# Half-wide gathered rows and an accumulating scatter in the expert part of a Macaron block

## The chip, the cores and the metric

The kernel runs on one core of a Trainium2 chip, in one launch. The metric is the device time of that core in microseconds (us).

## The reference, cut to what matters

The block computes x + 0.5 ffn(ln(x)), then adds causal attention with a relative bias, then adds 0.5 ffn(ln(x)) again, on 8192 tokens of 256 channels in float32. Both ffn calls have the same weights. One ffn is:

```python
y1 = _ln(x + _mha(x, ...), ln1_g, ln1_b)
y2 = _ln(y1 + _moe(y1, wg, w1, b1, w2, b2), ln2_g, ln2_b)   # then out = x + 0.5 * y2
# _moe: token -> its best of 8 experts, at most 1024 tokens each; others get 0
h = einsum('ecd,edf->ecf', disp, w1) + b1
y = einsum('ecf,efd->ecd', h, w2) + b2
out = where(keep, gate_val * y[slot], 0.0)
```

There is no nonlinearity between w1 and w2, so the kernel folds each expert into one 256x256 matrix.

## The kernel before, in words

`macaron` (L2422) runs `ffn` (turn 0, from the input to the scratch tensor x1), three stages of the causal attention, and `ffn` again (turn 1, from x2 to the output). Each stage ends with a barrier over the engines.

`ffn` (L943) has three parts.

1. `ffn_attention` (L295) goes over 16 groups of 512 tokens. It computes y1 and the router's logits. On GpSimd, `x_ahead` (L884) adds the halved ln2_b to the block's input. SyncE stores two things in token order into `rows`, a DRAM scratch tensor of 8192 rows of 2C floats: y1 into the first C columns (L340) and that residual part into the last C (L344).
2. VectorE works out a slot for every token (L1351 to L1435), sorted by expert, and with TensorE (L1271) its inverse `inv`: which token sits in slot i. In turn 0 alone, TensorE folds the weights meanwhile: `turn_w1` (L1238) and `product` (L1250) for each of 8 experts, from w1 and w2 tiles that SyncE loads; VectorE computes `bias_product` (L1441), ScalarE evacuates. In turn 1 the folded weights are loaded.
3. The expert loop goes over 16 groups of 4 tiles of 128 slots. GpSimd first issues all 64 gathers (L1094): each is one indirect DMA that fetches 128 rows of `rows`, 2 KB a row, by `inv` into the buffer `xs`. Then it issues 64 scatters (L1112), four when a group is finished (`s_fin`), each writing 128 rows of 1 KB to the result by `inv`. ScalarE copies the gathered y1 (`place`, L1147), evacuates its transpose (L1155), seeds the PSUM banks with the bias (L1162), takes the root (L1169) and normalises (L1173). TensorE transposes (L1228) and multiplies (L1321). VectorE adds the gated expert result and takes statistics (`sums`, L1463), the factors (L1487), and in `scale` (L1496) multiplies by ln2_g (L1498) and adds the gathered residual part (L1501). The order on VectorE in step n is sums(n), factors(n-1), scale(n-2). The first two and last two steps are unrolled, the middle is a hardware loop over pairs.

The first TensorE work behind the weights is L1318, which marks the PSUM banks; the loop can't start before it.

`xs` holds 16 groups of GT*2C floats in each partition, 128 KB. Before the gathers it is lent out: groups 0 to 7 to part 1 and to the tables of the inverse, 8 and 9 to the slot computation, 10 to 15 to the w1 and w2 tiles. So in turn 0 the gathers of groups 10 to 15 wait for the folding:

```python
for n in range(NG):
    if turn == 0 and n in (10, 11):
        pool.wait_ge(s_etps, 4 * (n - 3))
    if turn == 0 and n >= 12:
        pool.wait_ge(s_w12ps, n - 7)
        pool.wait_ge(s_acc, n - 7)
    gather(n)
```

`gather(n)` also waits until the gathers of group n-2 have landed. Before the first gather GpSimd waits until all stores of part 1 have landed (`stored`, L922), and behind the last scatter until all scatters have (L1114).

Of the kernel before, what the change touches and what calls it, by code (L numbers as in the profile page):

```python
# [291 lines left out]
            nc.tensor.transpose(core.ps[:, 7, 0:NE * FB], b1raw[:, :], core.ident[0:NE * FB, 0:NE * FB]).then_inc(s_b1ps, 1)  # L292


def ffn_attention(core, ph, lend, x, rows, logits, first, tables, early_loads):  # L295


    nc = core.nc
    xg = x.rearrange("(p t) c -> p (t c)", p=P)
    rowsg = rows.rearrange("(p t) c -> p t c", p=P)  # L300
    wide, kv, xs, ys, back = lend
    qT = wide.take(2, 2, GW)
    xin, xb, xres = (wide.take(2, GT, C) for _ in range(3))
# [35 lines left out]
    def sync(sp):  # L339
        def store(n, u):  # L340
            sp.wait_ge(s_y1, n + 1)
            sp.dma_start(rowsg[:, bass.ds(n * GT, GT), 0:C], y1[:, u, :, :]).then_inc(s_store[u], 16)

        def ahead(n, u):  # L344
            sp.wait_ge(s_xb, n + 1)
            sp.dma_start(rowsg[:, bass.ds(n * GT, GT), C:2 * C], xb[:, u, :, :]).then_inc(s_ahead[u], 16)

        def body(n, u):
            if not under(n, 2):
                sp.wait_ge(s_xres, n - 1)  # L350
                sp.wait_ge(s_xTps, 2 * n - 2)
            sp.dma_start(xin[:, u, :, :].rearrange("p t c -> p (t c)"),
                         xg[:, bass.ds(n * GT * C, GT * C)]).then_inc(s_load[u], 16)
            if not under(n, 1):
                ahead(n - 1, 1 - u)
            if not under(n, 4):
                store(n - 4, u)
            if n == NG - 1:
                early_loads(sp)
            if first and 2 <= n < 2 + len(tables):  # L360
                sp.dma_start(*tables[n - 2]).then_inc(core.tables, 16)
        each(NG, body)
        ahead(NG - 1, (NG - 1) % 2)
        for n in range(NG - 4, NG):
            store(n, n % 2)
        for u in range(2):
            sp.wait_ge(s_store[u], 16 * (NG // 2))
            sp.wait_ge(s_ahead[u], 16 * (NG // 2))
# [574 lines left out]
def ffn(core, name, x, rows, d, w12d, b12d, out, turn, tables):  # L943

    nc = core.nc
    FB = FF // P
    CT = TILES // NG * 2
    MINE = (2, 5)  # L950
    with Phase(core, name) as ph:
        logits = ph.sb("logits", [P, TILES, NE])

        def tile(n, *shape, dt=F32):
            return ph.sb(n, [P, *shape], dt)
        mx, se, first, keep, loc, rank, drop, dscan, t2, t3 = (tile(n, TILES) for n in (
            "mx", "se", "first", "keep", "loc", "rank", "drop", "dscan", "t2", "t3"))
        xs = ph.sb("xs", [P, NG, GT, 2 * C])
        flat = xs[:, :, :, :].rearrange("p g t c -> p (g t c)")
        ROWS = GT * 2 * C  # L960

        def lent(k, *shape):

            n, k = int(np.prod(shape)), int(k * ROWS)
            names = "abc"[:len(shape)]
            return flat[:, k:k + n].rearrange(f"p ({' '.join(names)}) -> p {' '.join(names)}", **dict(zip(names, shape)))

        CHUNKS = TILES // CT
        onb, ona = lent(0, CHUNKS, CT, P), lent(4, CHUNKS, CT, 2 * TILES)
        dif, ex, cand = (lent(8 + i / 4, TILES, NE) for i in range(3))  # L970
        hot, scan, a3, b3 = (lent(9 + i / 4, NE, TILES) for i in range(4))
        w1 = [lent(10 + i, KB, FF) for i in range(2)]
        w2 = [lent(12 + i, FB, C) for i in range(4)]
        onest = tile("onest", TILES)
        eidx, ebase, tot, cnt, free, fend, fbeg, off = (tile(n, NE) for n in (
            "eidx", "ebase", "tot", "cnt", "free", "fend", "fbeg", "off"))
# [28 lines left out]
                                                   ("rs", [P, 2, GT]), ("nb", [P, 2, GT])))  # L1005
        s_got, s_sent = core.indirect[0:2], core.indirect[2]
        got0, sent0 = turn * 16 * TILES // 2, turn * 16 * TILES
        s_tps, s_tsb, s_zps, s_sum, s_st, s_mv, s_ve, s_sd, s_inv2, s_rs, s_norm, s_scaled, s_fin, s_marked, s_seed = (
            ph.sem(x) for x in ("tps", "tsb", "zps", "sum", "st", "mv", "ve", "sd", "inv2", "rs", "norm", "scaled", "fin",
                                "marked", "seed"))  # L1010
        gnow = ph.sb("gnow", [P, 2, GT])
        s_gnow, s_mine, s_y1 = ph.sem("gnow"), ph.sem("mine"), ph.sem("y1")
# [31 lines left out]
        def load_w1(sp, e):  # L1044
            if e >= 2:
                sp.wait_ge(s_etps, 4 * (e - 1))
            sp.dma_start(w1[e % 2], d["L0_ffn_w1"][e, :, :].rearrange("(k p) f -> p k f", p=P)).then_inc(s_w1[e % 2], 16)

        def load_w2(sp, e):
            if e >= 4:  # L1050
                sp.wait_ge(s_w12ps, e - 3)
                sp.wait_ge(s_acc, e - 3)
            sp.dma_start(w2[e % 4], d["L0_ffn_w2"][e, :, :].rearrange("(k p) c -> p k c", p=P)).then_inc(s_w2[e % 4], 16)

        lend = (Lent(flat[:, 0:7 * ROWS]), Lent(w12[:, :, :].rearrange("p k c -> p (k c)")),
                Lent(xT[:, :, :, :].rearrange("p u k c -> p (u k c)")),
                Lent(y1[:, :, :, :].rearrange("p u t c -> p (u t c)")), Lent(flat[:, 7 * ROWS:8 * ROWS]))
        attend_sync, attend_tensor, attend_scalar, attend_vector, attend_gpsimd, over_yet, stored = ffn_attention(
            core, Phase(core, name + "_a", ph), lend, x, rows, logits, turn == 0, tables, early_loads)
        block = ph.block()  # L1060

        @block.sync
# [18 lines left out]
        @block.gpsimd  # L1081
        def _(pool):
            nc.gpsimd.iota(ei[:, :], pattern=[[1, NE]], base=0, channel_multiplier=0).then_inc(s_iota, 1)
            nc.gpsimd.iota(ib[:, :], pattern=[[1, P]], base=0, channel_multiplier=0).then_inc(s_ib, 1)
            nc.gpsimd.iota(ni[:, :], pattern=[[1, TILES]], base=0, channel_multiplier=TILES).then_inc(s_ni, 1)
            nc.gpsimd.memset(zero[:, :], 0.0).then_inc(s_zero, 1)
            attend_gpsimd(pool)

            def gather(n):
                if n >= 2:  # L1090
                    got(pool, n - 2, n % 2)
                for t in range(GT):
                    i = n * GT + t
                    pool.indirect_dma_start(xs[:, n, t, :], None, rows,  # L1094
                                            bass.IndirectOffsetOnAxis(ap=inv[:, i:i + 1], axis=0)
                                            ).then_inc(s_got[n % 2], 16)

            for u in range(2):
                stored(pool, u)
            pool.wait_ge(s_inv, 1)  # L1100
            for n in range(NG):
                if turn == 0 and n in (10, 11):
                    pool.wait_ge(s_etps, 4 * (n - 3))
                if turn == 0 and n >= 12:
                    pool.wait_ge(s_w12ps, n - 7)
                    pool.wait_ge(s_acc, n - 7)
                gather(n)
            for n in range(NG):
                pool.wait_ge(s_fin, n + 1)
                for t in range(GT):  # L1110
                    i = n * GT + t
                    pool.indirect_dma_start(out, bass.IndirectOffsetOnAxis(ap=inv[:, i:i + 1], axis=0),  # L1112
                                            xs[:, n, t, 0:C], None).then_inc(s_sent, 16)
            pool.wait_ge(s_sent, sent0 + 16 * TILES)  # L1114

        @block.scalar
# [226 lines left out]
        def _(dve):  # L1343
# [152 lines left out]
            def scale(n):  # L1496
                wait_apart(dve, s_norm, n + 1)
                nc.vector.tensor_tensor(all_rows(n, 0, C), all_rows(n, 0, C), over(core.rows["ln2_g"][:, :], GT, 1),  # L1498
                                        ALU.mult).then_inc(s_scaled, 1)
                wait_apart(dve, s_scaled, n + 1)  # L1500
                nc.vector.tensor_tensor(all_rows(n, 0, C), all_rows(n, 0, C), all_rows(n, C, 2 * C), ALU.add).then_inc(s_fin, 1)  # L1501

            def body(n, u):
                sums(n, u)
# [917 lines left out]
def macaron(nc, d, out):  # L2422
    def scratch(name, shape, dt=F32):
        return nc.dram_tensor(name, shape, dt, kind="Internal").ap()

    x = d["L0_attn_x"].rearrange("b t c -> (b t) c")
    y = out.rearrange("b t c -> (b t) c")
    x1, x2 = (scratch(n, (S, C)) for n in ("x1", "x2"))
    rows = scratch("rows", (S, 2 * C))
    w12d, b12d = scratch("w12d", (P, KB * NE * C)), scratch("b12d", (P, NE * C))  # L2430
    qd, kd = (scratch(n, (B * C, 3, T), BF16) for n in ("qparts", "kparts"))
    relrow = scratch("relrow", (AH, 2, 3 * P))
    neard = scratch("neard", (AH, P, PITCH))
    neardT = scratch("neardT", (AH, P, PITCH))
    lowd = scratch("lowd", (2 * B * NHG, LOW_PARTS, HG * T // 2), BF16)
    with ExitStack() as ctx:
        core = Core(nc, ctx)
        prepare(core, d, relrow)
        ffn(core, "ffn1", x, rows, d, w12d, b12d, x1, 0, distance_tables(relrow, neard, neardT))
        with Phase(core, "attention") as ph:  # L2440
            vall = ph.sb("vall", [P, B * NHG, QB, HG * AD])
            attention_qkv(core, x1, qd, kd, vall)
            attention_core(core, qd, kd, neard, neardT, lowd, vall)
            attention_out(core, x1, vall, x2)
        ffn(core, "ffn2", x2, rows, d, w12d, b12d, y, 1, ())
# [27 lines left out]
```

## Time and profile before

| | us |
|---|---|
| median of 3 runs | 2800.32 (2793.59 to 2802.8) |
| the profiled execution's own time | 2796.27 |
| its span | 2794.5 |
| busy: PE, DVE, ACT, POOL | 2350.3, 2150.2, 1657.6, 818.8 |
| indirect DMA issues on POOL: gathers, scatters | 122.8, 130.4 |

In the rows, POOL is GpSimd, DVE VectorE, ACT ScalarE, PE TensorE (PEld its weight loads) and SP SyncE. A row of a timeline has its start, its duration, the engine, the line, the operation, what it writes and reads, how often it stands there, and in brackets the idle time before it and what ended it. "issue" is time in which the engine waited for nothing that the profile shows.

### The profile page before, as it was taken

The numbers are of one execution on the slowest core, as the hardware profiler recorded it, in microseconds if no ns is written. First come the engines' busy times: TensorE is split into PE (matmuls) and PEld (weight loads), VectorE is DVE, ScalarE is ACT, GpSimd is POOL, SyncE is SP. The second block draws the span as 40 slices with busy tenths as digits, with TensorE's granted clock in tenths as the row PEclk, the third lists the DMA queues.
The fourth block names the chain that finished last, engine by engine and source line by source line (L and its number), as shares of the span: only waits on it lengthen the run. The fifth ranks groups of instructions, "written<-read, shape, count | busy, mean of one in ns | idle before, by whom it ended". The sixth has DMA issues, their size and how long they took to land. (4 is left out here: it accounts for less than half of the span.)

```text
span 2794.5 us, 47798 instructions
## 1 busy us (share of the span) xinstructions
PE 2350.3 (84%) x15864; PEld 1424.9 (51%) x15864; DVE 2150.2 (77%) x5653; ACT 1657.6 (59%) x3995; POOL 818.8 (29%) x853
## 2 busy tenths in 40 slices
PE   5999998867479969999999999999869999984263
PEld 4666665746345514444444444444646666663243
DVE  5888887727778869888898988997448888886076
ACT  3455453416534429999999999999215545442154
POOL 2243443263634420000000000000223344331735
PEclk8999999878789969999999999999989999996677
DMA  4132213382235464454554544542441121111712
GB/s 119 53 98 73 69 56 134 133 259 94 79 128 172 160 130 102 93 109 99 101 109 91 105 104 96 111 94 44 139 140 54 46 69 53 61 52 55 210 62 73
DMA packets 244680, 281.50 MB, mean 101 GB/s; under 512 B 41809, under 2 KB 212881, under 8 KB 243809
## 3 DMA queue, kind: packets, MB, share of 16 engines
q1 hardware_dynamic: 218192, 218.81, 30.7%
q0 software_dynamic: 16384, 50.35, 5.7%
q10 hardware_dynamic: 9872, 9.45, 1.0%
q8 instruction: 123, 2.02, 0.3%
q14 instruction: 109, 0.88, 0.1%
HBM read 190.63 MB, written 94.16 MB: 102 GB/s over the span
## 5 line engine op out<-in xcount | busy, mean ns | idle before, releaser
L2208 DVE CUSTOM_DVE_ANT_0 banks<-banks,attn_bias 128x128 f32<-128x128 f32 (+7 forms) x1024 | 759.9, 778 | 109.1 <-PE banks L1917 83.3
L2121 ACT ACTIVATE attn_probT<-banks 128x512 f32<-128x512 f32 x1152 | 622.6, 621 | 61.7 <-PE banks L1934 51.4
L1917 PE MATMUL banks<-attn_kst,attn_qst 96*128 96x512 bf16 (+3 forms) x1536 | 421.9, 336 | 22.9 <-DMA attn_kst<-kparts 12.7
L1934 PE MATMUL banks<-attn_qst,attn_kst 99*128 99x256 bf16 (+3 forms) x2176 | 410.8, 281 | 15.0 <-ACT attn_probT L2121 6.8
L1956 PE MATMUL banks<-attn_probT,attn_vb 128*32 128x256 f32 (+3 forms) x4352 | 316.0, 400 | 7.7 <-ACT attn_probT L2121 7.3
L1934 PEld LDWEIGHTS banks<-attn_qst,attn_kst 99*128 99x128 bf16 x2176 | 187.8, 98 | 168.5 <-ACT attn_probT L2121 54.5
L2266 POOL CAST attn_lowp<-attn_lowT 128x32 bf16<-128x32 f32 x64 | 13.4, 209 | 851.4 <-DVE attn_lowT L2216 851.4
L421 PE MATMUL banks<-ffn_xT,winT 128*128 128x512 f32 x512 | 250.9, 613 | 6.0 <-ACT ffn_w L621 2.9
L1917 PEld LDWEIGHTS banks<-attn_kst,attn_qst 96*128 96x128 bf16 x1536 | 117.5, 97 | 257.3 <-DVE attn_low L2208 159.2
L2109 ACT COPY banks<-attn_biasT 128x512 f32<-128x512 f32 x384 | 227.8, 628 | 28.3 <-DMA attn_biasT<-neardT 21.7
L881 POOL TENSOR_TENSOR ffn_xs<-ffn_xs,row_ffn_out 128x1024 f32<-128x1024 f32 x32 | 75.3, 2354 | 413.6 <-DVE ffn_xs L763 387.1
L591 ACT ACTIVATE ffn_xs<-banks,ffn_xs 128x128 f32<-128x128 f32 x512 | 182.4, 379 | 13.0 <-DVE ffn_xs L728 11.6
L1956 PEld LDWEIGHTS banks<-attn_probT,attn_vb 128*32 128x32 f32 x4352 | 106.2, 109 | 132.8 <-ACT attn_probT L2121 69.9
L630 ACT COPY ffn_xs<-banks 128x256 f32<-128x256 f32 x128 | 48.2, 377 | 203.6 <-PE banks L470 200.2
L1329 PE MATMUL banks<-ffn_w,ffn_xT 128*128 (+1 forms) x512 | 135.0, 419 | 40.3 <-issue 30.3
L1094 POOL DMA_INDIRECT ffn_xs<-rows,ffn_inv x128 | 122.8, 960 | 146.8 <-DVE ffn_inv L1435 94.1
L621 ACT ACTIVATE ffn_w<-banks,ffn_qk_b 64x512 f32<-64x512 f32 x128 | 87.3, 682 | 128.7 <-PE banks L421 127.9
L728 DVE TENSOR_REDUCE ffn_xs<-banks 128x4 f32<-128x512 f32 x128 | 88.5, 691 | 89.7 <-PE banks L450 89.7
L450 PEld LDWEIGHTS banks<-ffn_w,ffn_xs 128*128 128x128 f32 x1024 | 133.8, 198 | 23.7 <-issue 20.3
L450 PE MATMUL banks<-ffn_w,ffn_xs 128*128 128x128 f32 x1024 | 143.6, 285 | 0.8 <-DVE ffn_xs L750 0.8
L2208 DVE DVE_READ_ACCUMULATOR2_ANT attn_low<- 128x1 f32 x1024 | 144.3, 141 | 0.0
L736 DVE TENSOR_SCALAR ffn_xs<-ffn_xs 128x128 f32<-128x128 f32 x512 | 137.8, 331 | 4.5
(254 smaller groups left out, 4489.5 us busy)
## 6 DMA issues: line engine op xcount, KB each, us to landing
rows<-ffn_xs SPq DMA_DIRECT2D x64, 512.0 KB, 3.1
attn_qst<-qparts SPq DMA_DIRECT2D x384, 64.0 KB, 2.8
attn_kst<-kparts SPq DMA_DIRECT2D x192, 128.0 KB, 4.9
ffn_xs<-in_L_ffn_w_dram SPq DMA_DIRECT2D x16, 1024.0 KB
attn_biasT<-neardT SPq DMA_DIRECT2D x128, 128.0 KB, 4.9
attn_bias<-neard SPq DMA_DIRECT2D x128, 128.0 KB, 2.2
qparts<-qkv_part SPq DMA_DIRECT2D x32, 384.0 KB, 2.8
kparts<-qkv_part SPq DMA_DIRECT2D x32, 384.0 KB, 2.8
```

The source lines that it names most:

```text
L421: mm = nc.tensor.matmul(bank[QK], core.winT[:, k, j * P:(j + 1) * P], xT[:, u, k, :], start=(k == 0), stop=(k == KB - 1))
L450: mm = nc.tensor.matmul(bank[SC[t % 2]][:, h * P:(h + 1) * P], qT[:, u, h // 2, t * P:(t + 1) * P], kT[:, u, h, t * P:(t + 1) * P], start= ...
L591: ins = nc.scalar.activation(prob[:, t % 2, h, :], bank[SC[t % 2]][:, h * P:(h + 1) * P], ACT.Exp, bias=negm[:, t % 2, h:h + 1], scale=1.0 ...
L736: ins = nc.vector.tensor_scalar(prob[:, t % 2, h, :], prob[:, t % 2, h, :], rinv[:, t % 2, h:h + 1], None, ALU.mult)
L1094: pool.indirect_dma_start(xs[:, n, t, :], None, rows, bass.IndirectOffsetOnAxis(ap=inv[:, i:i + 1], axis=0)).then_inc(s_got[n % 2], 16)
L1329: mm = nc.tensor.matmul(part, xT[:, u, k, t * P:(t + 1) * P], w12[:, k, expert(n, u)], start=False, stop=(k == KB - 1), skip_group_check=True)
L1917: mm = nc.tensor.matmul(score[k % 2][:, a:e], qst[0:K6, u, half, hh, ii * P:(ii + 1) * P], kst[0:K6, u, hh, a:e], start=True, stop=True)
L1934: mm = nc.tensor.matmul(tbank[t % 3][:, at:at + nb * P], kst[:, u, hh, j * P:(j + 1) * P], qst[:, u, half, hh, x:x + nb * P], start=(k == ...
L1956: mm = nc.tensor.matmul(obank[32 * hh:32 * hh + 32, x:x + nb * P], vb[:, u, j, hh, :], probT[:, g % 2, i, at:at + nb * P], start=hh not in ...
L2109: nc.scalar.copy(tbank[t % 3].rearrange("p (a c) -> p a c", a=2), over(near[:, 0:2 * P], 2, 1)).then_inc(s_seed, 1)
L2121: nc.scalar.activation(probT[:, g % 2, i, 0:w], tbank[t % 3][:, 0:w], ACT.Exp, scale=-1.0).then_inc(s_exp, 1)
L2208: nc.vector.tensor_tensor_reduce(out=part, in0=part, in1=bias[:, hh, T - w:T], scale=1.0, scalar=BIG, op0=ALU.add, op1=ALU.min, accum_out= ...
```

## The change

`rows` has C columns and holds y1 alone. The residual part is stored in token order to the result of the ffn itself (x1 in turn 0, the output in turn 1). The gathers fetch 1 KB a row. VectorE's addition L1501 is gone with its semaphore. The scatters add to the result in DRAM instead of overwriting it. `xs` has half the size, and the tiles of the slot computation and of w1 and w2 are allocated beside it, so the waits of turn 0 ahead of the gathers of groups 10 to 15 are gone. The tables of the inverse still lie in `xs`.

```diff
-            sp.dma_start(rowsg[:, bass.ds(n * GT, GT), 0:C], y1[:, u, :, :]).then_inc(s_store[u], 16)
+            sp.dma_start(rowsg[:, bass.ds(n * GT, GT), :], y1[:, u, :, :]).then_inc(s_store[u], 16)
-            sp.dma_start(rowsg[:, bass.ds(n * GT, GT), C:2 * C], xb[:, u, :, :]).then_inc(s_ahead[u], 16)
+            sp.dma_start(outg[:, bass.ds(n * GT, GT), :], xb[:, u, :, :]).then_inc(s_ahead[u], 16)
...
-        xs = ph.sb("xs", [P, NG, GT, 2 * C])
+        xs = ph.sb("xs", [P, NG, GT, C])
...
-        onb, ona = lent(0, CHUNKS, CT, P), lent(4, CHUNKS, CT, 2 * TILES)
-        dif, ex, cand = (lent(8 + i / 4, TILES, NE) for i in range(3))
-        hot, scan, a3, b3 = (lent(9 + i / 4, NE, TILES) for i in range(4))
-        w1 = [lent(10 + i, KB, FF) for i in range(2)]
-        w2 = [lent(12 + i, FB, C) for i in range(4)]
+        before_rows = Lent(flat)
+        onb, ona = before_rows.take(CHUNKS, CT, P), before_rows.take(CHUNKS, CT, 2 * TILES)
+        dif, ex, cand = (tile(n, TILES, NE) for n in ("dif", "ex", "cand"))
+        hot, scan, a3, b3 = (tile(n, NE, TILES) for n in ("hot", "scan", "a3", "b3"))
+        w1 = [tile(f"w1_{i}", KB, FF) for i in range(2)]
+        w2 = [tile(f"w2_{i}", FB, C) for i in range(4)]
...
             for n in range(NG):
-                if turn == 0 and n in (10, 11):
-                    pool.wait_ge(s_etps, 4 * (n - 3))
-                if turn == 0 and n >= 12:
-                    pool.wait_ge(s_w12ps, n - 7)
-                    pool.wait_ge(s_acc, n - 7)
                 gather(n)
...
-                                            xs[:, n, t, 0:C], None).then_inc(s_sent, 16)
+                                            xs[:, n, t, :], None, compute_op=ALU.add).then_inc(s_sent, 16)
...
                 nc.vector.tensor_tensor(all_rows(n, 0, C), all_rows(n, 0, C), over(core.rows["ln2_g"][:, :], GT, 1),
-                                        ALU.mult).then_inc(s_scaled, 1)
-                wait_apart(dve, s_scaled, n + 1)
-                nc.vector.tensor_tensor(all_rows(n, 0, C), all_rows(n, 0, C), all_rows(n, C, 2 * C), ALU.add).then_inc(s_fin, 1)
+                                        ALU.mult).then_inc(s_fin, 1)
...
-    rows = scratch("rows", (S, 2 * C))
+    rows = scratch("rows", (S, C))
```

## Rows read from the trace of the kernel before

**Rows 1.** Engines' busy time by stretch; then granted clock, DMA share, GB/s

```profile
core 0: us, PE busy (x) PEld busy (x) DVE busy (x) ACT busy (x) POOL busy (x), PEclk, DMA share, GB/s
50.00:500.00 450.00, 410.71 (x2508) 287.95 (x2508) 370.16 (x1023) 218.16 (x754) 174.58 (x91) 0.97 0.26 82
580.00:600.00 20.00, 10.41 (x22) 5.03 (x20) 0.00 (x0) 0.00 (x0) 15.13 (x17) 0.50 0.75 223
2607.00:2617.00 10.00, 0.00 (x0) 0.00 (x0) 0.00 (x0) 0.00 (x0) 7.56 (x9) 0.50 0.72 207
2657.00:2667.00 10.00, 2.93 (x5) 1.15 (x4) 1.04 (x3) 0.00 (x0) 0.59 (x1) 0.50 0.20 59
2677.00:2757.00 80.00, 59.23 (x274) 47.41 (x273) 71.06 (x199) 57.43 (x112) 42.73 (x44) 0.93 0.20 72
```

**Rows 2.** Timeline of POOL, turn 1: first and last gather, first and last scatter

```profile
2577.76 1.09 POOL L1094 DMA_INDIRECT ffn_xs<-rows,ffn_inv  x1 [47.20 <-DVE ffn_inv L1435]
...
2656.65 0.95 POOL L1094 DMA_INDIRECT ffn_xs<-rows,ffn_inv  x1 [0.30 <-issue]
2678.54 1.00 POOL L1112 DMA_INDIRECT out_dram<-ffn_xs,ffn_inv  x1 [20.95 <-DVE ffn_xs L1501]
...
2786.10 0.97 POOL L1112 DMA_INDIRECT out_dram<-ffn_xs,ffn_inv  x1 [0.30 <-issue]
```

**Rows 3.** Timeline of POOL, turn 0: first and last gather, first and last scatter

```profile
540.65 1.44 POOL L1094 DMA_INDIRECT ffn_xs<-rows,ffn_inv  x1 [46.85 <-DVE ffn_inv L1435]
...
635.46 0.95 POOL L1094 DMA_INDIRECT ffn_xs<-rows,ffn_inv  x1 [0.30 <-issue]
659.19 1.01 POOL L1112 DMA_INDIRECT x<-ffn_xs,ffn_inv  x1 [22.78 <-DVE ffn_xs L1501]
...
765.52 0.97 POOL L1112 DMA_INDIRECT x<-ffn_xs,ffn_inv  x1 [0.30 <-issue]
```

**Rows 4.** A piece of the chain of waits, turn 1: start, us, what

```profile
2603.50 19.10 issue
```

**Rows 5.** Timeline of DVE, two steps of the expert loop

```profile
2700.71 0.16 DVE L1466 COPY ffn_gnow<-ffn_gates 128x4 f32 x1
...
2705.32 1.23 DVE L1498 TENSOR_TENSOR ffn_xs<-ffn_xs,row_ln_g 128x1024 f32 x1
2706.74 1.23 DVE L1501 TENSOR_TENSOR ffn_xs<-ffn_xs  x1 [0.20 <-issue]
2707.89 0.16 DVE L1466 COPY ffn_gnow<-ffn_gates 128x4 f32 x1
...
2714.95 0.16 DVE L1466 COPY ffn_gnow<-ffn_gates 128x4 f32 x1
```

**Rows 6.** Timeline of ACT, the same step

```profile
2704.96 0.21 ACT L1171 ACTIVATE ffn_ve<-ffn_ve 128x4 f32<-128x4 f32 x1 [1.67 <-issue]
...
2709.28 1.10 ACT L1166 COPY banks<-ffn_b 128x512 f32 x2
```

**Rows 7.** DMA queue of the gathers, 2577 to 2667: packets, MB, share

```profile
q0 software_dynamic: 5120, 16.78, 64.6%
```

**Rows 8.** DMA queue of the scatters, 2677 to 2757: packets, MB, share

```profile
q0 software_dynamic: 2112, 5.77, 20.3%
```

**Rows 9.** Timeline of PE, turn 1: the first products of the loop

```profile
2593.31 4.93 PE L1329 MATMUL banks<-ffn_w,ffn_xT 128*128 128x256 f32 x16
```

**Rows 10.** Timeline of PE, turn 0: three products, the banks' marks

```profile
548.26 7.07 PE L1257 MATMUL banks<-ffn_xs,ffn_xT 128*128 128x256 f32 x32
...
568.53 7.07 PE L1257 MATMUL banks<-ffn_xs,ffn_xT 128*128 128x256 f32 x32
...
611.59 7.07 PE L1257 MATMUL banks<-ffn_xs,ffn_xT 128*128 128x256 f32 x32
...
633.21 5.40 PE L1318 MATMUL banks<-ffn_w,ones 128*128 128x512 f32 x8 [0.56 <-issue]
```

**Rows 11.** Timeline, all engines: a scatter's issue beside VectorE's product

```profile
2761.79 1.22 DVE L1498 TENSOR_TENSOR ffn_xs<-ffn_xs,row_ln_g 128x1024 f32<-128x1024 f32 x1
2761.85 1.99 POOL L1112 DMA_INDIRECT out_dram<-ffn_xs,ffn_inv  x1 [0.30 <-issue]
```

More of the change, by code:

```diff
@@ L292, in _, with ffn_attention @@
             nc.tensor.transpose(core.ps[:, 7, 0:NE * FB], b1raw[:, :], core.ident[0:NE * FB, 0:NE * FB]).then_inc(s_b1ps, 1)
-def ffn_attention(core, ph, lend, x, rows, logits, first, tables, early_loads):
+def ffn_attention(core, ph, lend, x, rows, out, logits, first, tables, early_loads):
     nc = core.nc
     xg = x.rearrange("(p t) c -> p (t c)", p=P)
-    rowsg = rows.rearrange("(p t) c -> p t c", p=P)
+    rowsg, outg = (a.rearrange("(p t) c -> p t c", p=P) for a in (rows, out))
     wide, kv, xs, ys, back = lend
@@ L957, in ffn @@
             "mx", "se", "first", "keep", "loc", "rank", "drop", "dscan", "t2", "t3"))
-        xs = ph.sb("xs", [P, NG, GT, 2 * C])
+        xs = ph.sb("xs", [P, NG, GT, C])
         flat = xs[:, :, :, :].rearrange("p g t c -> p (g t c)")
[L960 to L966, printed above, removed]
-        CHUNKS = TILES // CT
-        onb, ona = lent(0, CHUNKS, CT, P), lent(4, CHUNKS, CT, 2 * TILES)
-        dif, ex, cand = (lent(8 + i / 4, TILES, NE) for i in range(3))
-        hot, scan, a3, b3 = (lent(9 + i / 4, NE, TILES) for i in range(4))
-        w1 = [lent(10 + i, KB, FF) for i in range(2)]
-        w2 = [lent(12 + i, FB, C) for i in range(4)]
+        CHUNKS = TILES // CT
+        before_rows = Lent(flat)
[4 more added lines that the diff above has]
+        w2 = [tile(f"w2_{i}", FB, C) for i in range(4)]
         onest = tile("onest", TILES)
@@ L1007, in ffn @@
         got0, sent0 = turn * 16 * TILES // 2, turn * 16 * TILES
-        s_tps, s_tsb, s_zps, s_sum, s_st, s_mv, s_ve, s_sd, s_inv2, s_rs, s_norm, s_scaled, s_fin, s_marked, s_seed = (
-            ph.sem(x) for x in ("tps", "tsb", "zps", "sum", "st", "mv", "ve", "sd", "inv2", "rs", "norm", "scaled", "fin",
+        s_tps, s_tsb, s_zps, s_sum, s_st, s_mv, s_ve, s_sd, s_inv2, s_rs, s_norm, s_fin, s_marked, s_seed = (
+            ph.sem(x) for x in ("tps", "tsb", "zps", "sum", "st", "mv", "ve", "sd", "inv2", "rs", "norm", "fin",
                                 "marked", "seed"))
@@ L1046, in load_w1 @@
                 sp.wait_ge(s_etps, 4 * (e - 1))
-            sp.dma_start(w1[e % 2], d["L0_ffn_w1"][e, :, :].rearrange("(k p) f -> p k f", p=P)).then_inc(s_w1[e % 2], 16)
+            sp.dma_start(w1[e % 2][:, :, :], d["L0_ffn_w1"][e, :, :].rearrange("(k p) f -> p k f", p=P)).then_inc(s_w1[e % 2], 16)
         def load_w2(sp, e):
@@ L1052, in load_w2 @@
                 sp.wait_ge(s_acc, e - 3)
-            sp.dma_start(w2[e % 4], d["L0_ffn_w2"][e, :, :].rearrange("(k p) c -> p k c", p=P)).then_inc(s_w2[e % 4], 16)
-        lend = (Lent(flat[:, 0:7 * ROWS]), Lent(w12[:, :, :].rearrange("p k c -> p (k c)")),
+            sp.dma_start(w2[e % 4][:, :, :], d["L0_ffn_w2"][e, :, :].rearrange("(k p) c -> p k c", p=P)).then_inc(s_w2[e % 4], 16)
+        LATE = 2 * GT * C
+        lend = (Lent(flat[:, :-LATE]), Lent(w12[:, :, :].rearrange("p k c -> p (k c)")),
                 Lent(xT[:, :, :, :].rearrange("p u k c -> p (u k c)")),
-                Lent(y1[:, :, :, :].rearrange("p u t c -> p (u t c)")), Lent(flat[:, 7 * ROWS:8 * ROWS]))
+                Lent(y1[:, :, :, :].rearrange("p u t c -> p (u t c)")), Lent(flat[:, -LATE:]))
         attend_sync, attend_tensor, attend_scalar, attend_vector, attend_gpsimd, over_yet, stored = ffn_attention(
-            core, Phase(core, name + "_a", ph), lend, x, rows, logits, turn == 0, tables, early_loads)
+            core, Phase(core, name + "_a", ph), lend, x, rows, out, logits, turn == 0, tables, early_loads)
         block = ph.block()
```

## The prediction

> **What bounds the kernel now.** I read the stage table first. In part 1 of an ffn TensorE is busy 411 of 450 us [rows 1]; the change adds or takes nothing on TensorE there, so I look only at the stretch behind `inv`, in both turns. The timeline of POOL cuts it in two. In turn 1 the 64 gathers go out back to back from 2577.8 to 2657.6, one in 1.25 us; the first scatter follows only at 2678.5, and the last issue ends at 2787.07, 108.5 us later, though 64 scatters at 1.275 us (0.97 and 0.30 of gap) take 81.6 [rows 2]. In turn 0 gathers run from 540.7 to 636.4, scatters from 659.2 to 766.5, 107.3 us [rows 3].
>
> Why are the scatters late? While gathers run, the other engines nearly stop: between 2607 and 2617 PE, DVE and ACT run nothing, with DMA 72% busy at 207 GB/s; in turn 0 from 580 to 600 DVE and ACT none [rows 1]. The chain of waits has a piece of 19.1 us there that it calls "issue" [rows 4]: nothing that the trace shows is awaited. I read this as instructions that don't arrive. Afterwards the expert loop runs at DVE's pace, 71 busy of 80 us [rows 1], one step in 7.18 us here [rows 5] (7.12 as the mean of two neighbours), and POOL waits for each group.
>
> **L1501 goes.** From the start of L1498 to that of L1501 is 1.42 us, so a step of DVE falls from 7.12 to 5.70 [rows 5]. Next in line are ACT, 5.42 us from its root to the end of its seeds [rows 6], and POOL, 5.1 us for four scatters. PE is busy 59 of 80 us, about 5.3 a step [rows 1]. So DVE keeps the pace, and 15 steps give 21.3 us where the scatters follow DVE. The first group is finished 1.4 earlier besides. POOL's own floor, 81.6, lies below 107.3 - 21.3 = 86.0.
>
> **The gathers fetch half.** Their number and issue time stay: 80 us for 64. The bytes don't: the gather queue now takes 64.6% of the engines' time for 16.78 MB in 90 us, the scatters with 1 KB rows 20.3% for 5.77 MB in 80 us [rows 7, 8]. Per MB that is 3.5 and 2.8 us of the 16 engines, so gathers of 8.4 MB at 1.25 us each make DMA 30 to 37% busy instead of 72%. Part 1, with DMA at 26% on average, has PE near full [rows 1], and the loop with 1 KB scatters at 20% runs without stalls. I take it that the stalls go. What is late next: in turn 1 the loop can then follow the gathers: its first products start at 2593.3 [rows 9], and at 5.7 us a step it has finished most groups when the last gather is issued at 2657.6. Then nothing stands between POOL and its scatters: they start at 2657.9 instead of 2678.5, 20.6 earlier, and take 81.6 instead of 108.5, 26.9 less. L1501's gain is inside this, not beside it. **Turn 1: -47.5.**
>
> The Trainium skill bears on the stall (Runtime: NRT & Kernel Launch, Instruction fetch mechanics): instructions come in 16 KiB blocks over a DMA queue, a cost it calls mostly hidden. By that alone the stalls would not be the gathers' doing, and the smaller rows would not help; that is the first rival below. Its page DMA: Bandwidth & Descriptors (Queues, rings and completion order) says that a DMA engine takes turns between queues packet by packet, which would make a fetch wait on 2 KB rows longer than on 1 KB rows. The trace agrees with the second as far as stalls and gathers coincide [rows 1, 4].
>
> **Turn 0.** Products of PE start at 548.3 and, two later, at 568.5, 10.1 us each; two more would put the last at 588.8, and it starts at 611.6 [rows 10]: 22.8 us of stall. From its start to the marks of the banks another 21.6 us pass for 7.1 of matmul and two bias steps; some 10 would do. Of these 34 I take 30 and leave 4 to the stretch in which w1 and w2 still load beside the gathers. Scatters then start at 659.2 - 30 - 1.4 = 627.8. POOL must be through its gathers: without the waits on the folding 540.7 + 80 = 621, so the removed waits are needed for this gain and give nothing alone. With 86.0 for the scatters: **-30 - 1.4 - 21.3 = -52.7.**
>
> **Port.** The loop now overlaps the gathers. A scatter issued 0.06 us after L1498's start took 1.99 us instead of 0.97 [rows 11]. One such product per group remains. Per group the issue costs 0 (no issue starts in it) to 1.02 more; half gives 8 us over 16 groups in turn 1, where POOL never rests. In turn 0 POOL has slack against 5.7. **+8.** On this the Trainium skill (SBUF — State Buffer, the list of practical consequences) infers that tensor_tensor doesn't stall descriptor generation. By it this term would be 0 and the sum 8 lower; the row speaks against it.
>
> **The scatter adds.** No row shows an accumulating DMA. From below: it can't be cheaper than a plain scatter, since it reads the destination besides: 0. From above: like a gather and a scatter in one, 0.97 more at each issue. Gather and plain scatter, which differ in direction, are 0.95 and 0.97 [rows 2]. I take the near row and 0.05 more. In turn 1 that is 64 x 0.05 = 3.2; in turn 0 it hides below DVE's 5.7 (room of 0.15 each). **+3.2.** On the DMA side a scatter takes 20.3% of 80 us over 44 scatters, 0.37 us of the engines' time against a pitch of 1.275 [rows 8]; even three times that is covered.
>
> **With one answer.** The two stores of part 1 keep their bytes and their number and become contiguous; DMA there is 26% busy, no one waits: 0 (if that cover were gone, POOL's first gather would wait, and it waits for `inv` now [rows 2, 3]). SyncE's queue has the same issues in the same order. The landing behind the last scatter stays.
>
> **Sum.** -47.5 - 52.7 + 8 + 3.2 = -89 against 2796.27, the profiled execution's own time: 2707. That execution is 4.05 us under the median of the runs shown, so I forecast 2711.
>
> **Rivals.** *The stalls stay.* They come with the gathers' number or with POOL at work, not with bytes; for it speaks that both stay the same and that PE runs 2.9 us of 10 and DVE 1.0 even after the last gather's issue, with DMA at 20% [rows 1]. Against: stretches with scatters of as many rows show none. Then turn 1 starts its scatters at 2677 and needs 108.5 - 21.3 = 87.2, and each turn gives 22.7: 2800.3 - 45 + 3 = 2758. Chance 0.30.
>
> *The adding scatter is dear.* Its place is POOL's queue, behind the last gather, where nothing hides it. Call p the pitch of scatters. Turn 1 then ends its issues at 2657.9 + 8 + 64p, turn 0 at 627.8 + 64p; together these reach today's 2787.07 + 766.49 at p = 2.03, so from an issue of 1.73 us on the change loses. At the upper bound p = 2.25 it costs 28 on balance: 2828. The same holds if the DMA engines need 2.03 us for one, 5.5 times today's 0.37. For: it must read first. Against: gather and scatter cost POOL alike. Chance 0.12 for slower; about break-even 0.04.
>
> *Part of each:* some stalls stay in turn 0 (turn 1 hides them under POOL's scatters), or an issue of 0.2 to 0.4 more. 2730 to 2760, inside the range; it shares the remaining chance with the forecast: forecast 0.40, this 0.14.
>
> The range: 2692 (no port term, all 34 of turn 0, no price for adding) to 2778 (stalls stay and adding costs 0.15 to 0.2 an issue). Left out are a dear scatter and no change, about 0.2. A measurement of this kernel can tell about 0.3%, 8 us, from no change. Faster by more 0.84, within 0.04, slower 0.12.
>
> **What would show it.** Right: gathers at a pitch of 1.25 with DMA near 35%, DVE and ACT at work among them, no piece of "issue" over 5 us; in turn 1 the first scatter within 1 us of the last gather and 64 issues in about 85 us; DVE's step near 5.7. The step on the stalls is wrong if rows like those at 2607 stand there again; the step on the scatter if its issue is over 1.1 us or its queue's share over 60%. Slower than 2792 would make the whole wrong.

## The result, and the profile after

The changed kernel takes 2854.11 us (2850.97 to 2855.75) beside 2801.48 for the kernel before on the same chip (2793.59 to 2802.8): a ratio of 1.0193, 95% interval 1.0171 to 1.0214. It is 53 us slower, and 76 above the top of the forecast range. The whole prediction is wrong in sign.

The page of the changed kernel: span, busy times, the queue of the indirect DMAs (packets, MB, share of the 16 engines).

```profile
span 2854.0 us, 47711 instructions
PE 2348.4 (82%) x15864; PEld 1427.1 (50%) x15864; DVE 2118.4 (74%) x5621; ACT 1657.6 (58%) x3995; POOL 897.0 (31%) x853
q0 software_dynamic: 24576, 33.57, 7.4%
```

DVE has lost 32 us of work and the queue 17 MB, as planned. POOL has gained 78 us. The stage table of the changed kernel, columns as in [rows 1]:

```profile
580.00:600.00 20.00, 3.34 (x9) 1.46 (x8) 0.00 (x0) 0.00 (x0) 15.13 (x17) 0.50 0.36 105
600.00:620.00 20.00, 3.89 (x7) 1.90 (x7) 0.00 (x0) 0.00 (x0) 15.12 (x17) 0.50 0.36 105
2660.00:2680.00 20.00, 1.96 (x8) 1.57 (x8) 3.08 (x11) 1.50 (x3) 15.12 (x16) 0.50 0.37 105
2740.00:2760.00 20.00, 15.12 (x73) 12.46 (x70) 16.23 (x53) 14.02 (x28) 16.88 (x11) 0.91 0.62 69
```

The gathers keep their pitch of 1.25 us and DMA falls to 36%, both as forecast. But DVE and ACT still stand still from 580 to 620 and PE nearly so. In the last line the scatters keep DMA 62% busy, where it was 20%.

POOL's timeline of the changed kernel: first and last gather and first and last scatter of turn 1, the rows that answer to [rows 2].

```profile
2623.59 1.09 POOL L1089 DMA_INDIRECT ffn_xs<-rows,ffn_inv  x1 [47.22 <-DVE ffn_inv L1425]
...
2702.51 0.95 POOL L1089 DMA_INDIRECT ffn_xs<-rows,ffn_inv  x1 [0.30 <-issue]
2722.96 1.62 POOL L1102 DMA_INDIRECT out_dram<-ffn_xs,ffn_inv  x1 [19.51 <-DVE ffn_xs L1488]
...
2846.49 1.55 POOL L1102 DMA_INDIRECT out_dram<-ffn_xs,ffn_inv  x1 [0.31 <-issue]
```

Two things went other than forecast. POOL still waits 19.5 us for VectorE between its last gather and its first scatter. And a scatter's issue takes 1.55 us, not 0.97. By line, over both turns (nanoseconds min/median/max, then the starts):

```profile
L1102 POOL DMA_INDIRECT x<-ffn_xs,ffn_inv x64: 1556/1561/2378, 686.9 to 811.5; - x64
L1102 POOL DMA_INDIRECT out_dram<-ffn_xs,ffn_inv x64: 1552/1553/2062, 2723.0 to 2846.5; - x64
```

**Where the 59.5 us between the two spans lie.** In turn 0 the first scatter comes at 686.9 instead of 659.2 [rows 3]: +27.7. The stretch from there to the end of the last issue is 126.2 instead of 107.3: +18.9. In turn 1, counted from its first gather, the first scatter comes 1.4 earlier and the stretch behind it takes 125.1 instead of 108.5: +16.6. The stages between are 0.7 shorter, the tail behind the last issue 1.5. Of the 27.7, 1.7 lie ahead of the first gather, which comes at 542.30 instead of 540.65 [rows 3]. So 35 us lie in the scatters and 28 ahead of the first scatter of turn 0.

**The stalls of turn 1 did not change.** VectorE's long pauses during the gathers, timeline of the changed kernel:

```profile
2647.52 0.17 DVE L1456 COPY ffn_gnow<-ffn_gates 128x4 f32<-128x4 f32 x1 [24.80 <-DMA ffn_xs<-rows,ffn_inv]
...
2667.74 0.88 DVE L1462 SCALAR_TENSOR_TENSOR ffn_xs<-banks,ffn_gnow,ffn_xs 128x256 f32<-128x256 f32 x2 [19.15 <-remote]
...
2710.51 0.17 DVE L1456 COPY ffn_gnow<-ffn_gates 128x4 f32<-128x4 f32 x1 [39.58 <-remote]
```

The same instructions of the kernel before:

```profile
2602.37 0.22 DVE L1466 COPY ffn_gnow<-ffn_gates 128x4 f32<-128x4 f32 x1 [25.45 <-DMA ffn_xs<-rows,ffn_inv]
...
2622.60 0.88 DVE L1472 SCALAR_TENSOR_TENSOR ffn_xs<-banks,ffn_gnow,ffn_xs 128x256 f32<-128x256 f32 x2 [19.10 <-issue]
...
2664.68 0.17 DVE L1466 COPY ffn_gnow<-ffn_gates 128x4 f32<-128x4 f32 x1 [39.09 <-remote]
```

25.45 and 24.80, 19.10 and 19.15, 39.09 and 39.58: within 0.7 us the same pauses at half the bytes.

The prediction read these pauses as instructions that don't arrive. The DMA view has queues of kind "instruction" (q8 and q14, 232 packets over the kernel before). From 2600 to 2665 in the kernel before, and from 2645 to 2711 in the changed one, it lists no packet of theirs. Its only queue is the gathers', here in the kernel before and then in the changed one:

```profile
q0 software_dynamic: 3832, 12.55, 66.6%
```

```profile
q0 software_dynamic: 2305, 6.29, 33.3%
```

Yet VectorE goes on inside these stretches, at 2622.60 and 2664.68, at 2667.74 and 2710.51. So no instruction packet that the view records ends the second or the third of the pauses. That speaks against the reading; how the instructions reach their engines beyond these packets, no run shows.

**In turn 0 the stall grew.** PE's timeline of the changed kernel, to be read beside [rows 10]:

```profile
549.90 7.07 PE L1247 MATMUL banks<-ffn_w,ffn_xT 128*128 128x256 f32 x32
...
621.52 0.59 PE L1247 MATMUL banks<-ffn_w,ffn_xT 128*128 128x256 f32 x1 [2.21 <-issue]
624.32 0.59 PE L1247 MATMUL banks<-ffn_w,ffn_xT 128*128 128x256 f32 x1 [2.21 <-issue]
...
629.23 9.35 PE L1247 MATMUL banks<-ffn_w,ffn_xT 128*128 128x256 f32 x25 [1.52 <-issue]
...
640.60 7.07 PE L1247 MATMUL banks<-ffn_w,ffn_y 128*128 128x256 f32 x32
647.94 7.07 PE L1247 MATMUL banks<-ffn_w,ffn_xT 128*128 128x256 f32 x32
...
662.04 5.66 PE L1308 MATMUL banks<-ffn_w,ones 128*128 128x512 f32 x8 [0.56 <-issue]
```

From 572 to 629 PE gets a single matmul every 0.7 to 2.8 us. It is back at its pace at 629.2, 5 us behind the end of the gathers at 624.0. From 555 to 639 the DMA view lists no instruction packet here either. The banks' marks come at 662.0 instead of 633.2 [rows 10]. In the kernel before POOL met its waits on the folding on the way:

```profile
606.73 0.94 POOL L1094 DMA_INDIRECT ffn_xs<-rows,ffn_inv  x1 [4.72 <-remote]
...
631.71 0.94 POOL L1094 DMA_INDIRECT ffn_xs<-rows,ffn_inv  x1 [4.75 <-issue]
```

PE's row there:

```profile
604.21 7.11 PE L1257 MATMUL banks<-ffn_xs,ffn_y 128*128 128x256 f32 x18 [0.82 <-issue]
```

PE had run one to three matmuls at a time since 581; from 604.2, inside the first of these two pauses, it runs 18 together and then the full product at 611.59 [rows 10], beside the gathers that go on from 606.7. Two traces suggest that the removed waits had ended the stall; they don't show it.

### The profile page after: what moved, and what is told of

Read it like the earlier page. It is cut to its first block and busy times, and to the rows that moved or that the text cites. A ratio compares the mean times of both kernels' runs of the same rounds, so it can differ in the third digit from the quotient of the medians.

```text
span 2854.0 us, 47711 instructions
## 1 busy us (share of the span) xinstructions
PE 2348.4 (82%) x15864; PEld 1427.1 (50%) x15864; DVE 2118.4 (74%) x5621; ACT 1657.6 (58%) x3995; POOL 897.0 (31%) x853
## 3 DMA queue, kind: packets, MB, share of 16 engines
q1 hardware_dynamic: 193616, 218.81, 29.6%
q0 software_dynamic: 24576, 33.57, 7.4%
```

## The experiments

Two theories stood for the scatter. The add costs POOL time at the issue, or the engines can't keep up and POOL is held back. For the stalls there were three: they follow the gathers' bytes, their unbroken stream, or neither. The experiments below ran on chips that the record numbers 8, 1, 4 and 7. For the comparison it gives no number; that it was a fifth chip is taken from the times. **On none of the four does the kernel before show the stalled time**: it takes about 2730 there, not 2801, and its profile on chip 8 has no stall. Chip, time and the place where the program was loaded can all have differed, so "the first chip" below stands for the conditions of the comparison. Each time below is therefore beside the kernel before on its own chip. What the runs settle is the scatter, VectorE and POOL's queue; of the expectations' halves on stalls nothing could be tried.

### The add alone

`a_plain`: the changed kernel, its scatters plain. The residual part is left out of the result.

```diff
-                                            xs[:, n, t, :], None, compute_op=ALU.add).then_inc(s_sent, 16)
+                                            xs[:, n, t, :], None).then_inc(s_sent, 16)
```

> The changed kernel with plain scatters: they overwrite the result, so the residual part is left out of it. Theory (the addition makes the scatter dear at its issue): the issue falls from 1.56 to about 0.97 us and the pitch from 1.87 to 1.28; the scatters then follow VectorE at about 6 us a group, some 91 us in each turn instead of 126 and 125, so about 69 less than the changed kernel: 2785. The stalls beside the gathers stay as they are. Rival (the pitch comes from the smaller buffer or the narrow rows, not from the addition): the issue stays at 1.56 and the time at 2854.

Measured: 2709.13 beside 2729.53, ratio 0.9928 (0.9911 to 0.9944). POOL's timeline of this kernel, turn 1: first and last gather, first and last scatter.

```profile
2527.45 1.09 POOL L1089 DMA_INDIRECT ffn_xs<-rows,ffn_inv  x1 [47.19 <-DVE ffn_inv L1425]
...
2610.41 0.94 POOL L1089 DMA_INDIRECT ffn_xs<-rows,ffn_inv  x1 [0.30 <-issue]
2611.66 1.00 POOL L1102 DMA_INDIRECT out_dram<-ffn_xs,ffn_inv  x1 [0.30 <-issue]
...
2695.85 0.97 POOL L1102 DMA_INDIRECT out_dram<-ffn_xs,ffn_inv  x1 [0.30 <-issue]
```

No gap ahead of the first scatter, and 85.2 us for the 64. This is the flow that the prediction drew for turn 1. To price the add, the unchanged text of both kernels was run on the chip of `a_plain`:

> The kernel before, unchanged, for a profile beside the others on the chip that runs them. The last runs had the kernel before at 2730 instead of 2801, and no stalls beside the gathers. Theory (the stalls belong to the chip or to where the program lies in it, not to the kernel's bytes): where it takes about 2730 its profile shows PE, DVE and ACT at work while gathers run, and where it takes about 2800 it shows them standing still. Rival (the 70 us lie elsewhere, in the attention): the stalls beside the gathers are there at either time.

> The changed kernel, unchanged, on the same chip. Theory without stalls: the old waits on the folding don't bind, so it equals the version that had them back, 2777, 1.018 of the kernel before: all of it the dearer scatter. With stalls as on the first chip: 2854. Rival (the removed waits matter without stalls too): more than 5 above 2777.

Measured: `before_again` 2731.12 beside 2730.38, ratio 1.0002 (0.9992 to 1.0013), span 2729.9. `after_again` 2775.7 beside 2730.38, ratio 1.0161 (1.0139 to 1.0182), span 2774.1. Its turn 1 on POOL, last gather and then first and last scatter:

```profile
2643.88 0.95 POOL L1089 DMA_INDIRECT ffn_xs<-rows,ffn_inv  x1 [0.30 <-issue]
2645.13 1.63 POOL L1102 DMA_INDIRECT out_dram<-ffn_xs,ffn_inv  x1 [0.30 <-issue]
...
2766.59 1.55 POOL L1102 DMA_INDIRECT out_dram<-ffn_xs,ffn_inv  x1 [0.30 <-issue]
```

From first gather to the end of the last issue `after_again` takes 207.1 us and `a_plain` 169.4, in turn 0 210.2 and 176.3. The add costs 37.7 and 33.9 us. 64 scatters at 1.56 instead of 0.97 make 37.8. The whole cost of the add is in POOL's queue.

### Is it the engines or the issue?

`a_narrow`: the changed kernel, each adding scatter with 512 B a row. The second half of each row is left out.

```diff
-                    pool.indirect_dma_start(out, bass.IndirectOffsetOnAxis(ap=inv[:, i:i + 1], axis=0),
-                                            xs[:, n, t, :], None, compute_op=ALU.add).then_inc(s_sent, 16)
+                    pool.indirect_dma_start(out.rearrange("s (h c) -> (s h) c", h=2), bass.IndirectOffsetOnAxis(ap=inv[:, i:i + 1], axis=0),
+                                            xs[:, n, t, 0:C // 2], None, compute_op=ALU.add).then_inc(s_sent, 16)
```

> The changed kernel with adding scatters of 512 B rows: half of each finished row is added, to a half row of the result, so the result is left incomplete. Theory (the dearer issue is work of GpSimd for each row, about 1.6 times that of a plain row, whatever its length): the issue stays at 1.56 us, the pitch at 1.87, and the time is that of the changed kernel on the same chip; only the scatter queue's share of the DMA engines falls, from 60% to 35 to 50%. Rival (the issue waits for the DMA engines, which carry three times the packets of a plain scatter): the issue falls below 1.3 us and the time by over 20.

Measured, two executions: 2775.0 beside 2728.82, ratio 1.0169 (1.012 to 1.0218). The line of its scatters in turn 0, then the queue in `a_narrow` from 2660 to 2740:

```profile
L1102 POOL DMA_INDIRECT x<-ffn_xs,ffn_inv x64: 1556/1562/2390, 623.4 to 748.3; - x64
```

```profile
q0 software_dynamic: 6188, 2.82, 39.5%
```

The same queue in `after_again`, 2660 to 2740:

```profile
q0 software_dynamic: 6174, 5.62, 62.4%
```

And with plain scatters in `before_again`, 2640 to 2720:

```profile
q0 software_dynamic: 2880, 7.87, 27.6%
```

Half the bytes bring the share from 62.4 to 39.5% and leave the issue at 1.56. So the engines don't set the pace, the issue does. An adding scatter makes 144 packets, with 512 B rows too, and a plain one 48 (24576 and 12288 packets over the two whole kernels, 6144 of them the gathers'). Of each, 16 are small ones of 4 B. The other 128 of the adding scatter carry one row each, the 32 of the plain one four rows of 1 KB. Whether the issue's 0.59 us goes with these 96 packets is not shown; gathers of 2 KB rows make 80 packets, those of 1 KB rows 48, and both issue in 0.95 us.

### VectorE's addition alone

`b_noadd`: the kernel before without L1501. The residual part is gathered and not added.

```diff
-                                        ALU.mult).then_inc(s_scaled, 1)
-                wait_apart(dve, s_scaled, n + 1)
-                nc.vector.tensor_tensor(all_rows(n, 0, C), all_rows(n, 0, C), all_rows(n, C, 2 * C), ALU.add).then_inc(s_fin, 1)
+                                        ALU.mult).then_inc(s_fin, 1)
```

> The kernel before without VectorE's addition L1501 (the residual part, gathered as before in 2 KB rows, is left out of the result). Theory (the bytes of the gathers are worth nothing; what the change gains is VectorE's addition): without stalls it equals the changed kernel with plain scatters, 2709, within 4, 20 below the kernel before, because POOL's own 162 us a turn then bound it. With stalls: about 45 below the kernel before. Rival (the bytes count): it stays over 10 above the plain version's 2709.

Measured: 2715.11 beside 2730.38, ratio 0.9943 (0.9925 to 0.9961). VectorE's first operation of two steps in turn 0, and its one longer wait between them:

```profile
650.12 0.16 DVE L1466 COPY ffn_gnow<-ffn_gates 128x4 f32 x1
...
651.65 0.88 DVE L1472 SCALAR_TENSOR_TENSOR ffn_xs<-banks,ffn_gnow,ffn_xs 128x256 f32 x2 [0.29 <-PE banks L1329]
...
656.21 0.16 DVE L1466 COPY ffn_gnow<-ffn_gates 128x4 f32 x1
```

A step takes 6.09 here; six steps from 644.28 to 680.35 average 6.01. In `before_again` six from 643.47 to 686.21 average 7.12. The gain is 14.3 us in turn 0 and 1.2 in turn 1, where POOL's queue is the bound already. `a_plain` is 6 us below `b_noadd`, between the 4 of the theory and the 10 of its rival; their intervals overlap. By POOL's rows 4.6 of it lie in turn 0, where the gathers take 83.4 us instead of 89.3, and 0.5 in turn 1. The rest of the change, half the gathered bytes above all, is thus worth about 6 us where nothing stalls, and that isn't clear of noise.

### The removed waits

`a_gated` is the changed kernel with the waits on the folding back; `a_plain_gated` the same with plain scatters, without the residual part.

```diff
             for n in range(NG):
+                if turn == 0 and n in (10, 11):
+                    pool.wait_ge(s_etps, 4 * (n - 3))
+                if turn == 0 and n >= 12:
+                    pool.wait_ge(s_w12ps, n - 7)
+                    pool.wait_ge(s_acc, n - 7)
                 gather(n)
```

> The changed kernel with the waits on the folding put back ahead of the gathers of groups 10 to 15 of turn 0. Theory (an unbroken stream of indirect DMAs on GpSimd, whatever its bytes, keeps instructions from the other engines, and the old waits broke it twice): the folding runs on at each pause, the first scatter of turn 0 comes about 28 us earlier, near 659, and the time is about 2827. Rival (turn 0 stalls for a fixed time because of the code it enters, or the folding waits for its weights): 2854, within 5.

> The changed kernel with plain scatters and with the removed waits on the folding back; the residual part is left out of the result. Theory: where no stalls come, the waits cost nothing, since POOL never meets them: 2709 beside a kernel before of 2730, as without the waits, and 0.3 us between last gather and first scatter. Where the kernel before takes 2800, with stalls: the waits pause the gathers in turn 0 and the folding catches up, so the first scatter comes at 654 to 660 instead of the 687 of the changed kernel, and the scatters behind it take about 95: turn 0 ends at 750 to 760, turn 1 as in the changed kernel less 16: about 2750. Rival, with stalls: the waits are not what ends a stall in turn 0; then the first scatter comes at 680 to 690 with them too, and the time is 28 more, about 2780.

> The changed kernel with the removed waits back and its adding scatters, again on the chip of this job. Where no stalls come: 2776, the changed kernel's own time. Where the kernel before takes 2800, with stalls: theory that the removed waits are what ended the stall of turn 0: first scatter of turn 0 at 654 to 660, total 2826 (2854 less 28); rival that they had no part in it: 2854 and a first scatter at 687.

Measured: `a_gated` 2777.49 beside 2729.53, ratio 1.018 (1.0163 to 1.0197), and on another chip as `a_gated_2` 2776.97 beside 2728.24, ratio 1.0178 (1.0161 to 1.0195). `a_plain_gated` there 2707.57, ratio 0.9922 (0.9905 to 0.9938). These are the times of `after_again` and `a_plain`. Without stalls the waits cost and give nothing. Whether they end a stall needs a chip that stalls, and neither of these two did.

### Other ways to break the stream of gathers

`a_drain` and `b_drain`: each kernel, with the gathers of a group waiting until the group before has landed, not the last but one.

```diff
-                if n >= 2:
-                    got(pool, n - 2, n % 2)
+                if n >= 1:
+                    got(pool, n - 1, (n - 1) % 2)
```

> The changed kernel, each group's gathers issued only when those of the group before have landed (instead of two before). Theory of the unbroken stream: gathers take some 7.5 us a group, 120 in all, but the pauses let instructions through, so that folding and loop run beside them and no engine stands still for over 5 us; turn 0 scatters from about 662 (25 earlier), turn 1 about 20 later: about 2845. Rival (the stalls belong to the code, not to the stream): the stalls stay and gathers end 40 later in each turn, 2880 to 2930.

> The kernel before with the same edit: each group's gathers wait for the landing of the group before. Theory of the unbroken stream: no long stalls; the scatters begin at about 661 in turn 0 and 20 later than now in turn 1, but then run at POOL's own 82 us instead of 107: about 2770. Rival (stalls belong to the code): 2830 to 2880.

Measured: `a_drain` 2837.18, ratio 1.0397 (1.038 to 1.0415); `b_drain` 2797.13, ratio 1.0251 (1.0234 to 1.0268), both beside 2729.53. Each group of gathers now waits for a landing: `b_drain`'s take 141.8 us in turn 0, 89.6 without the edit, where 120 was expected; `a_drain`'s take 121.5. A drain is a dear way to make room.

`b_inter`: the kernel before, gathering 8 groups ahead and then one group of gathers and one of scatters in turn.

```diff
-            for n in range(NG):
+            def fetch(n):
...
+            AHEAD = 8
+            for n in range(AHEAD):
+                fetch(n)
...
+                if n >= 1 and n + AHEAD - 1 < NG:
+                    fetch(n + AHEAD - 1)
```

> The kernel before with another order on GpSimd: the gathers of 8 groups first, then in turn one more group's gathers and one finished group's scatters. Theory: with stalls, the scatters' waits break the stream of gathers, so that it gains 20 to 60 on the kernel before; without stalls VectorE's 7.1 us a group bounds the loop and nothing changes, 2730 within 8. Rival (mixing makes each group wait for its gathers behind the scatters of an earlier one): 10 to 30 slower.

Measured: 2746.45 beside 2730.38, ratio 1.0058 (1.004 to 1.0076). In turn 0 the last issue ends at 756.9 instead of 736.9. POOL stands at the first finished group, which comes late behind the folding, with the second half of its gathers still to issue. That is the rival's range of 10 to 30 slower.

`a_pause`: the changed kernel, with five dependent operations of POOL behind the gathers of groups 3, 7 and 11.

```diff
                 gather(n)
+                if n in (3, 7, 11):
+                    for _ in range(5):
+                        nc.gpsimd.tensor_tensor(rest[:, :], core.ones[:, 0:GT], core.mhalf[:, :], ALU.pow).then_inc(s_rest, 1)
+                        rested[0] += 1
+                        pool.wait_ge(s_rest, rested[0])
```

> The changed kernel with three pauses of GpSimd among the gathers, behind groups 3, 7 and 11, each of five dependent small operations of about 1 us. On a chip without stalls (the kernel before near 2730): theory, GpSimd's queue alone bounds both turns, so each turn gets longer by all of its pauses, about 16, and the time is 2776 + 32 = 2808; rival, the expert loop or the DMA engines bound it, and the pauses are hidden: under 2790. On a chip with stalls (the kernel before near 2800): the pauses let instructions through, and it is 15 to 50 faster than the changed kernel's 2854 there; if it isn't, breaks in the stream are not what ends a stall.

Measured: 2808.27 beside 2730.67, ratio 1.0287 (1.027 to 1.0305). Its first pause, POOL's timeline:

```profile
564.09 5.46 POOL L1101 TENSOR_TENSOR ffn_rest<-ones,mhalf 128x4 f32<-128x4 f32 x5
```

Six pauses of 5.46 us are 32.8. The measured time is 32.6 above `after_again`, which ran on another chip with the kernel before at the same 2730. With the expensive scatter behind it, every microsecond on POOL's queue is one at the end, in both turns.

## Why the prediction was wrong

**"The gathers fetch half", wrong.** "I take it that the stalls go" is the first step that failed: the cost of the stalls was put at nothing. On the chip of the comparison the pauses of turn 1 kept their length at half the DMA share. Of the 20.6 us that the first scatter of turn 1 was to come earlier, 1.4 came; in turn 0 it was to come 31.4 earlier and came 27.7 later. On the others they are absent with 2 KB rows. `before_again` in two stretches of turn 0 and one of turn 1, columns as in [rows 1] (the DMA share adds up the packets' times and can pass 1):

```profile
560.00:580.00 20.00, 16.62 (x89) 14.32 (x88) 7.93 (x17) 3.64 (x7) 14.09 (x16) 1.00 1.04 381
580.00:600.00 20.00, 17.28 (x88) 15.02 (x86) 12.14 (x27) 5.78 (x10) 15.43 (x16) 1.00 0.83 264
2580.00:2600.00 20.00, 15.23 (x72) 11.93 (x71) 17.43 (x53) 15.63 (x31) 15.15 (x16) 0.93 0.69 201
```

PE is 76 to 86% busy with DMA at 69 to 104%, where [rows 1] had PE at half with 75% in turn 0 and at nothing with 72% in turn 1. Of the three pauses of turn 1 the first is mostly no stall, as the same instruction of `before_again` waits 19.94 us for its first products:

```profile
2570.49 0.17 DVE L1466 COPY ffn_gnow<-ffn_gates 128x4 f32<-128x4 f32 x1 [19.94 <-PE banks L1329]
```

Behind it VectorE has no pause over 1.5 us there until the gathers end; the other two, of 19 and 39 us, are absent. Bytes are neither needed for a stall nor enough. I had inferred a cause from two things that coincide in one trace, and stall and gathers coincide whatever the cause. Nor do narrower rows shorten a packet: [rows 7] has 5120 packets, 1024 of them of 4 B, for 16.78 MB, and the changed kernel's turn 1 has 3072, again 1024 of 4 B, for 8.39 MB. The others are of 4 KB in both, so a fetch that took turns with them would wait as long on either. The Trainium skill calls instruction fetch mostly hidden (Runtime: NRT & Kernel Launch, Instruction fetch mechanics). The four chips without stalls agree with that; the first, with pauses of 19 and 39 us, would not, if fetch is what they are. The instruction queues above speak against fetch. What differs between the first chip and the others, no run shows.

**"The scatter adds", mis-sized: forecast 0.05 us an issue, measured 0.59.** It lies inside my bound of 0.97. I took the value of the nearest rows, and those were of DMAs that only copy. A gather and a plain scatter cost alike because both copy; they say nothing of an operation that does both. The term was +3.2 and is 38 in turn 1. In turn 0 I let it hide under VectorE's pace, and 34 show: at a pitch of 1.86, four scatters take 7.4 us, more than any step of VectorE.

**The rivals were priced one at a time.** The break-even issue of 1.73 us assumed that the stalls go and earn 70 us first. With the stalls in place the same sum reads 2677 + 64p in turn 1 and 657.8 + 64p in turn 0 against 2787.07 + 766.49. That gives p = 1.71, an issue of 1.41, and 1.56 loses. Without stalls in the first place, `before_again` spends 105.2 and 85.0 us on its scatters. Their 64p each gives p = 1.49, an issue of 1.19, or 1.25 if the gathers' 8 us are counted, and 1.56 loses again. The two doubtful steps together decided the sign, and no case joined them. A slip besides: the low end of the range, worked out as it says, is 2696 and not 2692, as the 4.05 us of the profiled execution was left out; it decided nothing.

**"Turn 0", wrong.** I wrote that the removed waits "are needed for this gain and give nothing alone". POOL was through its gathers at 624.0, near my 621, but PE had starved until then and the first scatter came at 686.9, not 627.8. On the first chip the first scatter came 27.7 us later instead; that the missing waits did this is argued from the two traces. On the others they are worth nothing, shown by three runs.

**"L1501 goes", right in kind.** The step falls by 1.1 us rather than 1.42, to 6.0 and not 5.70. VectorE now waits 0.29 us for a bank of PE in the step of `b_noadd` above, so PE sets a part of it. It gives 14 us in turn 0 and 1 in turn 1, as POOL's floor is next; the prediction had said that the gain of turn 1 would be "inside this, not beside it".

**"Port", right.** In `a_plain` the gathers of turn 1 take 83.9 us against 79.8 with nothing beside them [rows 2], and the scatters 85.2 against 81.6: 7.7, forecast 8. All engines of `a_plain` in that turn, a gather issued during VectorE's product:

```profile
2584.97 1.23 DVE L1488 TENSOR_TENSOR ffn_xs<-ffn_xs,row_ln_g 128x1024 f32 x1
...
2585.25 1.76 POOL L1089 DMA_INDIRECT ffn_xs<-rows,ffn_inv  x1 [0.30 <-issue]
```

Where the loop already overlaps the gathers, the kernel before pays for this too: 85.8 us for its gathers in `before_again`. The Trainium skill's inference (SBUF — State Buffer, practical consequences) that tensor_tensor leaves descriptor generation alone doesn't hold in this row: 1.76 against 0.95.

**POOL's queue as the floor, right**, and it is what made the rest cost so much. `a_pause` measures it: 32.6 us for 32.8.

**A coincidence to set aside.** `a_plain`, 2709, is 2 us off the forecast of 2711. Its gain is 20 us from a kernel before of 2730, not 89 from 2800.

**What stays open.** Why the first chip stalls, and whether a pause in the gathers ends a stall; with it, the cause of the 28 us of turn 0, half of the loss there. No kernel that stores the full result beat the kernel before. The three faster ones (`a_plain`, `a_plain_gated`, `b_noadd`) leave the residual part out.

## What to carry to other kernels

Before work is moved into a queue that already sets the end, price one instance of the new operation on that queue by a run of its own: the 1.23 us saved per group on VectorE here cost 4 x 0.59 on POOL. When two steps of a sum are doubtful, work out their joint case and its break-even, not each alone. A stall in which nothing is awaited is a fact of the one place where it was seen until a second chip shows it; don't build the larger half of a gain on it.

## What was not expected of the hardware

- The same program takes 2801 us in the comparison and 2728 to 2731 on chips 8, 1, 4 and 7 (medians). Of the 64.6 us between two spans (2794.5 and 2729.9) 29.6 lie in turn 0 up to its last issue, 38.2 in turn 1 from its first gather to the last issue; the stages between are 3 us longer on the faster chip. The whole difference is in the stretches of gathers and scatters.
- An indirect DMA that adds costs POOL 1.56 us an issue for 128 rows, a copying one 0.97, and rows of 512 B cost as much as rows of 1 KB. Plain gathers of 1 and 2 KB rows both cost 0.95.
- The adding scatter makes three times the packets, one for each row, and takes 60 to 62% of the 16 engines at a pitch near 1.9 us. At a pitch of 1.3 us, plain ones take 28%.
